# A graph attention layer: the loading queue asks for the first slab of weights when the second left half tile of x has landed instead of the first

## The chip, the cores and the metric

The kernel runs on one core of a Trainium2 chip. The metric is the device time in microseconds (us) of the whole kernel, as the median of several runs. One more run was recorded by the hardware profiler; its rows are used below.

## What is computed

x has 384 rows (nodes) of 1024 features. The reference, cut to what matters:

```python
h = jnp.maximum(_layernorm(x, axis=-1), 0.0)
q, k, v = h @ wq.T + bq, h @ wk.T + bk, h @ wv.T + bv
q2, k2, v2 = q @ wiq.T + biq, k @ wik.T + bik, v @ wiv.T + biv    # 16 heads of 64
mask = full((N, N), -inf).at[src, dst].set(softplus(edge_type_weights)[edge_type - 1])
scores = einsum('hnd,hmd->hnm', q2, k2) / 8 + mask                # diagonal always set
out = einsum('hnm,hmd->hnd', softmax(scores), v2)                 # 6528 edges
return x + out @ wo.T + bo
```

All in float32. The kernel gets the precision by splitting every operand into a rounded part ("hi") and a remainder ("lo") and doing three products, hi by hi, lo by hi and hi by lo, for each one.

## The kernel before

**Tiles and slabs.** x is three tiles of 128 rows (t = 0, 1, 2), each fetched in two half tiles of 512 columns, 256 KB each: left halves by the queue of SyncE (line 289), right halves by the queue of ScalarE (line 470). Each has its own semaphore, `x_in[t][0]` for the left and `x_in[t][1]` for the right. The seven weight matrices are 56 slabs of 128x1024 floats, 512 KB each, that go through three landing buffers (`raw`). A slab is used in order: slab 0 makes the first product tile, slab 1 the second, and so on. Each slab is first split: ScalarE writes the hi part (line 456), then VectorE (line 712) or GpSimd (line 374) writes the lo part. Slab 0 is split in halves: ScalarE makes hi of the left half (line 467), VectorE hi of the right half (line 695), GpSimd both lo parts (line 384).

**The loading queue.** SyncE does nothing but wait for semaphores and issue transfers, in program order. After the three left half tiles of x its loop over the slabs (lines 297 to 336) issues slab 0, slab 1, then five small tables (edge weights, biases, two row tables of the edges, column tables of the edges), slab 2, and two 576 KB fills of the table in memory into which the mask is scattered. From slab 3 on, the issue of a slab waits until the slab three places before it has been split (line 300). The first slab has a wait of its own (line 304): SyncE issues nothing more until a half tile of x has landed.

**The head of the kernel.** VectorE takes the statistics of each half tile (line 679) and joins those of a tile (lines 683 and 685). GpSimd turns the variance into a scale (line 367). VectorE makes the shift of tile t from it (line 626); that instruction is placed behind the statistics of the left half of tile t + 1. ScalarE normalises tiles 0 and 1 with one instruction each (line 476). Tile 2 is finished by VectorE and ScalarE in parts (lines 689, 693 and 482). TensorE turns the tiles (line 894), ScalarE and VectorE split the turned h into `a_hi` and `a_lo` (lines 486 and 725), and the first product tile (lines 922 to 929) begins. Before that TensorE does matmuls on constants to fill its time (line 890). ScalarE's order in the head is: tile 0, tile 1, hi of the left half of slab 0, tile 2, the turned h, with the hi part of slab 1 behind the fifth piece of h, and then slab 2.

**After the head.** TensorE goes through 8 product tiles for v, 8 slabs for v2, 16 tiles for q and k, 16 for q2 and k2 between the heads of the attention, and the output product. Product tile 3, for example, needs the lo part of slab 3 and the evacuated result of tile 1 (the waits in `tile`, lines 859 to 863). Beside this VectorE works out which edge wins for each cell, GpSimd scatters 51 columns of edge values and 3 of the diagonal in two chains (lines 396 and 403), and the finished mask (line 720) is first used with the first scores (line 769).

Of the kernel before, what the change touches and what calls it, by code (L numbers as in the profile page):

```python
# [66 lines left out]
def tiles_of(group):  # L67
    return range(group * EG, min((group + 1) * EG, ET))


def gat_kernel(nc, slabs, x, edge_cols, edge_rows, edge_weights, biases, bo, out):
    with ExitStack() as ctx:
# [3 lines left out]
        def sem(name):  # L76
            return ctx.enter_context(nc.semaphore(name))
# [71 lines left out]
        def key_copy(pos):  # L149

            first, n = [(work2, 0), (work2, 4), (work2, 8), (work, 0), (work, 4), (work, 8), (prob, 19), (prob, 23),
                        (prob, 3), (prob, 7), (prob, 11), (prob, 15), (prob, 0)][pos], len(tiles_of(UNIT_ORDER[pos])) * P
            flat = prob[:, :, :, :].rearrange("p a t n -> p (a t n)") if first[0] is prob else first[0]
            return flat[:, first[1] * P:first[1] * P + n]

        def cell_rows(c):

            return cells[c][0:N * N, :].rearrange("(t p n) a -> p t (n a)", p=P, n=N)
# [18 lines left out]
        x_in = [[sem(f"x_in{t}_{b}") for b in range(2)] for t in range(NT)]  # L177
# [83 lines left out]
        def wait_lo(eng, s):  # L261

            eng.wait_ge(slab_lo_dve if lo_by_vector(s) else slab_lo, lo_count(s))
# [22 lines left out]
        @block.sync  # L286
        def _(sp_eng):
            for t in range(NT):
                sp_eng.dma_start(x_sb[:, t, 0:HALF], x[t * P:(t + 1) * P, 0:HALF]).then_inc(x_in[t][0], 16)  # L289
            def load_keys(pos):  # L290

                unit = UNIT_ORDER[pos]
                part = key_rows[0:1, unit * EG * P:(unit * EG + len(tiles_of(unit))) * P]
                sp_eng.dma_start(key_copy(pos), part.to_broadcast([P, len(tiles_of(unit)) * P])).then_inc(
                    keys_in[pos], 16)

            for s in range(SLABS):
                if s >= RAW:

                    wait_lo(sp_eng, s - RAW)  # L300
                    if s == RAW:
                        sp_eng.wait_ge(half_lo, 1)
                if s == 0:
                    sp_eng.wait_ge(x_in[0][0], 16)
                sp_eng.dma_start(raw[:, s % RAW, :], slabs[s]).then_inc(slab_in[s % RAW], 16)
                if s == 1:
                    sp_eng.dma_start(ew[:], edge_weights.rearrange("(a n) -> a n", a=1).to_broadcast([P, 4])).then_inc(
                        ew_in, 16)
                    sp_eng.dma_start(bias[:], biases).then_inc(small_in, 16)
                    for i in range(2):  # L310
                        sp_eng.dma_start(rows_i[:, i, :], edge_rows[i * DST_ROW:i * DST_ROW + ET, :]).then_inc(rows_in, 16)
                    sp_eng.dma_start(cols_i[:], edge_cols).then_inc(edges_in, 16)
                if s == 2:
                    for c in range(2):
                        sp_eng.wait_ge(fill_ok, c + 1)
                        sp_eng.dma_start(cell_rows(c), prob[:, c]).then_inc(filled, 16)
                if s == 4:
                    sp_eng.wait_ge(key_row_ok, 1)
                    sp_eng.dma_start(key_rows[0, :].rearrange("(t e) -> t e", e=P), key_row[:]).then_inc(keys_out, 16)
                if 6 <= s < 4 + GROUPS:  # L320
                    if s == 6:
                        sp_eng.wait_ge(keys_out, 16)
                    elif s == 10:
                        sp_eng.wait_ge(filled, 32)
                    if s < 8:
                        load_keys(2 * (s - 6))
                        load_keys(2 * (s - 6) + 1)
                    else:
                        load_keys(s - 4)
                if s == Q0 + 2:  # L330

                    sp_eng.wait_ge(h_turned, KT)
                    sp_eng.wait_ge(later_ok, 3 * EG)
                    for t in range(NT):
                        sp_eng.dma_start(y[:, t, :], x[t * P:(t + 1) * P, :]).then_inc(y_in, 16)
                    sp_eng.dma_start(bo_sb, bo.rearrange("(a n) -> a n", a=1).to_broadcast([P, F])).then_inc(y_in, 16)
            for i, (_, n, cols_out, _) in enumerate(out_pieces):
                sp_eng.wait_ge(out_ok, i + 1)
                sp_eng.dma_start(out[n * P:(n + 1) * P, cols_out], y[:, n, cols_out]).then_inc(stored, 16)
            sp_eng.wait_ge(stored, 16 * len(out_pieces))  # L340
# [110 lines left out]
        def _(act):  # L451
# [6 lines left out]
            def tile_hi_part(t):  # L458
                hi, _, b, psum = tile_place(t)
                act.wait_ge(slab_used, slab_of(t) + 1)  # L460
                nc.scalar.activation(hi, psum[:, 0:N], ACT.Identity, bias=bias[:, b:b + 1]).then_inc(tile_hi, 1)  # L461
# [137 lines left out]
        def _(dve):  # L599
# [241 lines left out]
            for i, (_, n, cols_out, psum) in enumerate(out_pieces):  # L841
                dve.wait_ge(out_done, i + 1)
                nc.vector.tensor_tensor(y[:, n, cols_out], psum, y[:, n, cols_out], ALU.add).then_inc(out_ok, 1)
# [283 lines left out]
```

## Time and profile before

| | |
|---|---|
| median of 3 runs | 295.54 us (295.51 to 296.37) |
| the profiled execution | 295.47 us |
| its span in the trace | 293.7 us |
| TensorE busy (matmul) | 287.4 us, 98% of the span |
| TensorE's share of the chain that ended last | 95% |
| transfers' share of that chain | 2% |
| VectorE, ScalarE, GpSimd busy | 60%, 52%, 51% |
| moved by the DMA engines | 40.84 MB, 139 GB/s on the mean |
| one slab, from issue to landing | 3.4 us (median of 56) |

The span is the stretch in which the engines' instructions lie; the profiled execution's own time is 1.8 us longer. "Busy" is the time in which at least one instruction of the engine was running. The chain that ended last is followed back from the last instruction, each time to what released it, so an engine's share of it says how much of the time it decided. TensorE's granted clock was at full speed, 2.4 GHz, in the whole stretch up to the last few us.

### The profile page before, as it was taken

The page shows a single profiled execution, that of the slowest core. Times are in us where ns is not written, and L with a number is a line of the kernel's source. Part 1 is how long each engine was busy: PE and PEld are TensorE (multiplying, and loading weights), DVE is VectorE, ACT ScalarE, POOL GpSimd, SP SyncE. Part 2 cuts the span into 40 slices and gives each one's busy share as a digit, 9 for nine tenths or more (in the row PEclk, how much of TensorE's full clock was granted, in tenths as well). Part 3 has the DMA queues.
Part 4 walks back from the last instruction along what each step waited for, and adds up shares of the span by engine and source line. Part 5 has one row for each costly group of instructions (what it writes and reads, how often), then busy time and mean ns, then how long its engine had stood idle before and what let it go on. Part 6 is the DMA issues. An engine that isn't in the chain of part 4 may idle for free.

```text
span 293.7 us, 4994 instructions
## 1 busy us (share of the span) xinstructions
PE 287.4 (98%) x1813; PEld 266.4 (91%) x1813; DVE 176.7 (60%) x475; ACT 153.5 (52%) x288; POOL 150.7 (51%) x153
## 2 busy tenths in 40 slices
PE   6899999999999999999999999999999999999996
PEld 3699998888899999999999999999999997888885
DVE  4999778786544534454467766665747475835241
ACT  2876443152523443244324685969687879874100
POOL 6552455543464455545300797758393939874000
PEclk9999999999999999999999999999999999999999
DMA  7978955749733443334654043140403132400032
GB/s 257 332 230 264 315 191 180 232 153 301 270 105 117 139 143 136 91 134 145 182 193 145 0 141 106 46 144 0 145 10 136 41 106 71 144 1 2 0 143 71
DMA packets 15818, 40.84 MB, mean 139 GB/s; under 512 B 3481, under 2 KB 4914, under 8 KB 15794
## 3 DMA queue, kind: packets, MB, share of 16 engines
q1 hardware_dynamic: 13346, 38.53, 39.2%
q0 software_dynamic: 2016, 1.21, 1.8%
q10 hardware_dynamic: 432, 0.79, 0.7%
q8 instruction: 14, 0.23, 0.3%
q14 instruction: 10, 0.08, 0.1%
HBM read 37.71 MB, written 2.81 MB: 138 GB/s over the span
## 4 chain that ended last, share of the span: by engine, by line
PE 95%; DMA 2%; ACT 1%; DVE 0%; SPq 0%; issue 0%
PE banks L849 27%; PE banks L850 26%; PE banks L851 26%; PE banks L966 5%; PE banks L1009 3%; PE banks L1010 3%; PE banks L981 3%; DMA x_sb<-in_x 2%; PE banks L994 1%; PE banks L894 1%; PE banks L922 1%; PE banks L929 0%; PE banks L923 0%; ACT x_sb L476 0%; SPq L289 0%; DVE stats L679 0%
## 5 line engine op out<-in xcount | busy, mean ns | idle before, releaser
L403 POOL DMA_INDIRECT cells<-value,cell x51 | 54.8, 1074 | 59.2 <-DMA cells<-value,cell 45.9
L456 ACT ACTIVATE w_hi<-raw 128x1024 fp32r<-128x1024 f32 x51 | 53.8, 1055 | 17.5 <-PE banks L851 17.3
L849 PE MATMUL banks<-a_hi,w_hi 128*128 128x384 f32 x184 | 61.5, 334 | 0.0
L850 PE MATMUL banks<-a_hi,w_lo 128*128 128x384 f32 x184 | 61.5, 334 | 0.0
L851 PE MATMUL banks<-a_lo,w_hi 128*128 128x384 f32 x184 | 61.5, 334 | 0.0
L712 DVE TENSOR_TENSOR w_lo<-raw,w_hi 128x1024 fp32r<-128x1024 f32 x36 | 44.0, 1223 | 12.6 <-ACT w_hi L456 12.5
L429 POOL TENSOR_SCALAR prob<-prob,row_inv 128x384 f32<-128x384 f32 x36 | 22.5, 640 | 43.6 <-DVE row_inv L779 43.6
L374 POOL TENSOR_TENSOR w_lo<-raw,w_hi 128x1024 fp32r<-128x1024 f32 x15 | 36.0, 2404 | 0.9 <-ACT w_hi L456 0.9
L849 PEld LDWEIGHTS banks<-a_hi,w_hi 128*128 128x128 f32 x184 | 34.5, 188 | 0.1
L850 PEld LDWEIGHTS banks<-a_hi,w_lo 128*128 128x128 f32 x184 | 34.5, 188 | 0.0
L851 PEld LDWEIGHTS banks<-a_lo,w_hi 128*128 128x128 f32 x184 | 34.5, 188 | 0.0
L783 DVE TENSOR_TENSOR pt_lo<-banks,pt_hi 128x384 fp32r<-128x384 f32 x48 | 23.8, 551 | 13.3 <-ACT pt_hi L548 13.1
L461 ACT ACTIVATE b_hi<-banks,bias 128x384 fp32r<-128x384 f32 x16 | 9.3, 581 | 35.0 <-PE banks L851 35.0
L534 ACT ACTIVATE prob<-prob,neg_max 128x384 f32<-128x384 f32 x36 | 21.8, 606 | 9.2 <-DVE neg_max L769 9.2
L548 ACT ACTIVATE pt_hi<-banks 128x384 fp32r<-128x384 f32 x48 | 20.1, 491 | 5.6 <-PE banks L1010 4.5
L849 PE MATMUL banks<-c_hi,w_hi 128*128 128x384 f32 x64 | 22.2, 346 | 0.0
L700 DVE SCALAR_TENSOR_TENSOR b_lo<-banks,bias,b_hi 128x384 fp32r<-128x384 f32 x16 | 9.9, 617 | 20.1 <-ACT b_hi L461 20.1
L849 PE MATMUL banks<-b_hi,w_hi 128*128 128x384 f32 x64 | 21.9, 343 | 0.0
L851 PE MATMUL banks<-b_lo,w_hi 128*128 128x384 f32 x64 | 21.4, 335 | 0.0
L851 PE MATMUL banks<-c_lo,w_hi 128*128 128x384 f32 x64 | 21.4, 334 | 0.0
L850 PE MATMUL banks<-c_hi,w_lo 128*128 128x384 f32 x64 | 21.4, 334 | 0.0
L850 PE MATMUL banks<-b_hi,w_lo 128*128 128x384 f32 x64 | 21.4, 334 | 0.0
(146 smaller groups left out, 610.1 us busy)
## 6 DMA issues: line engine op xcount, KB each, us to landing
raw<-in_slabs SPq DMA_DIRECT2D x56, 512.0 KB, 3.4
work<-key_rows SPq DMA_DIRECT2D x6, 256.0 KB, 5.3
prob<-key_rows SPq DMA_DIRECT2D x6, 256.0 KB, 3.8
x_sb<-in_x SPq DMA_DIRECT2D x3, 512.0 KB, 6.0
out_y<-x_sb SPq DMA_DIRECT2D x5, 256.0 KB, 2.1
cells<-prob SPq DMA_DIRECT2D x2, 576.0 KB, 7.9
cells<-value,cell POOLq DMA_INDIRECT x51, 2.6
x_sb<-in_x ACTq DMA_DIRECT2D x3, 256.0 KB, 4.3
```

The lines of the kernel that those rows point to most:

```text
L374: nc.gpsimd.tensor_tensor(lo, raw[:, s % RAW, :], hi.bitcast(F32), ALU.subtract).then_inc(slab_lo, 1)
L403: nc.gpsimd.indirect_dma_start(out=cells[c][:, :], out_offset=bass.IndirectOffsetOnAxis(ap=cell[:, t:t + 1], axis=0), in_=value[:, t:t + 1 ...
L429: nc.gpsimd.tensor_scalar(probs[j % 2][x][:, n, :], probs[j % 2][x][:, n, :], row_inv[:, j % 2, c:c + 1], 1.0, ALU.mult, ALU.mult).then_in ...
L456: nc.scalar.activation(split_place(s)[0], raw[:, s % RAW, :], ACT.Copy).then_inc(slab_hi, 1)
L534: nc.scalar.activation(probs[j % 2][x][:, n, :], probs[j % 2][x][:, n, :], ACT.Exp, scale=-1.0, bias=neg_max[:, j % 2, c:c + 1], accum_out ...
L548: nc.scalar.activation(pt_as_placed(pt_hi, h, m), pt_place(h, m), ACT.Copy).then_inc(pt_hi_ok, 1)
L712: nc.vector.tensor_tensor(lo, raw[:, s % RAW, :], hi.bitcast(F32), ALU.subtract).then_inc(slab_lo_dve, 1)
L783: nc.vector.tensor_tensor(pt_as_placed(pt_lo, h, m), pt_place(h, m), pt_as_placed(pt_hi, h, m).bitcast(F32), ALU.subtract).then_inc(pt_lo_ ...
L849: nc.tensor.matmul(psum, w[0], a[0], start=first, stop=False)
L850: nc.tensor.matmul(psum, w[1], a[0], start=False, stop=False)
L851: return nc.tensor.matmul(psum, w[0], a[1], start=False, stop=last)
L966: mm = nc.tensor.matmul(score_bank(2 * n + x)[:, 0:N], q[own, turn, m], k[own, turn, :], start=(p == 0), stop=(p == 2))
```

## The change

In its loop over the slabs SyncE waits ahead of slab 0 on another semaphore: on that of the left half of tile 1 instead of the left half of tile 0. Nothing else changes: the same transfers are issued by the same queues in the same order.

```diff
                 if s == 0:
-                    sp_eng.wait_ge(x_in[0][0], 16)
+                    sp_eng.wait_ge(x_in[1][0], 16)
                 sp_eng.dma_start(raw[:, s % RAW, :], slabs[s]).then_inc(slab_in[s % RAW], 16)
```

## Rows read from the trace of the kernel before

**Rows 1.** Waits of TensorE in the whole span: total us, times, longest.
```profile
PE banks L894 <- ACT x_sb L476: 0.9, 2, 0.6
PE banks L922 <- ACT a_hi L486: 0.2, 1, 0.2
```

**Rows 2.** Chain that ended last, its head: start us, us, what.
```profile
1.70 6.04 DMA x_sb<-in_x
12.10 0.41 PE banks L922
```

**Rows 3.** Timeline of SyncE's queue, the head: start us, us, instruction.
```profile
3.97 0.80 SPq L305 DMA_DIRECT2D raw<-in_slabs  x2
...
7.27 0.43 SPq L305 DMA_DIRECT2D raw<-in_slabs  x1
7.75 0.96 SPq L316 DMA_DIRECT2D cells<-prob  x2
13.68 3.60 SPq L305 DMA_DIRECT2D raw<-in_slabs  x2
```

**Rows 4.** DMA issues: x left of tile 1 (1.2 us), of tile 2 (1.7 us); last, us to landing.
```profile
x_sb<-in_x SPq DMA_DIRECT2D x1, 256.0 KB, 4.2
...
x_sb<-in_x SPq DMA_DIRECT2D x1, 256.0 KB, 6.0
```

**Rows 5.** DMA issues: slabs 0, 2, 3, 4 (issued at 4.0, 7.3, 13.7, 17.0 us); second fill.
```profile
raw<-in_slabs SPq DMA_DIRECT2D x1, 512.0 KB, 5.1
...
raw<-in_slabs SPq DMA_DIRECT2D x1, 512.0 KB, 6.6
...
raw<-in_slabs SPq DMA_DIRECT2D x1, 512.0 KB, 4.2
...
raw<-in_slabs SPq DMA_DIRECT2D x1, 512.0 KB, 3.3
...
cells<-prob SPq DMA_DIRECT2D x1, 576.0 KB, 8.5
```

**Rows 6.** Busy time by stretch; last three columns: granted clock, DMA share, GB/s moved.
```profile
1.00:7.00 6.00, 4.55 (x18) 2.24 (x18) 2.86 (x7) 1.70 (x2) 4.13 (x13) 1.00 0.83 288
7.00:7.74 0.74, 0.32 (x2) 0.00 (x0) 0.52 (x3) 0.74 (x1) 0.07 (x1) 1.00 1.06 418
```

**Rows 7.** Timeline of VectorE, the head and first use of the mask.
```profile
7.76 0.69 DVE L679 BATCH_NORM_STATS2 stats<-x_sb 128x6 f32<-128x512 f32 x1 [0.18 <-DMA x_sb<-in_x]
8.37 0.14 DVE L626 SCALAR_TENSOR_TENSOR shift<-mean_var,rstd 128x1 f32<-128x1 f32 x1
...
16.24 0.69 DVE L618 TENSOR_SCALAR sp<-ew 128x4 f32<-128x4 f32 x1
...
23.34 0.62 DVE L700 SCALAR_TENSOR_TENSOR b_lo<-banks,bias,b_hi 128x384 fp32r<-128x384 f32 x1
...
152.75 1.36 DVE L720 SCALAR_TENSOR_TENSOR work<-prob 128x1152 f32<-128x1152 f32 x1
...
159.33 0.55 DVE L769 CUSTOM_DVE_ANT_0 prob<-banks,work 128x384 f32<-128x384 f32 x1
```

**Rows 8.** Timeline of GpSimd, second tile's scale and first scatter.
```profile
7.67 0.55 POOL L367 TENSOR_TENSOR rstd<-var_eps,minus_half 128x1 f32<-128x1 f32 x1 [1.31 <-DVE var_eps L685]
...
22.30 1.26 POOL L396 DMA_INDIRECT cells<-sp,self_cell  x1 [3.20 <-issue]
```

**Rows 9.** Timeline of ScalarE, the instructions that read slabs 0 to 3.
```profile
9.70 0.62 ACT L467 ACTIVATE w_hi<-raw 128x512 fp32r<-128x512 f32 x1
...
13.33 1.10 ACT L456 ACTIVATE w_hi<-raw 128x1024 fp32r<-128x1024 f32 x1
...
15.39 1.13 ACT L456 ACTIVATE w_hi<-raw 128x1024 fp32r<-128x1024 f32 x1
...
17.93 1.06 ACT L456 ACTIVATE w_hi<-raw 128x1024 fp32r<-128x1024 f32 x1
```

**Rows 10.** Timeline of TensorE, the first matmul of product tile 3.
```profile
25.43 0.33 PE L849 MATMUL banks<-a_hi,w_hi 128*128 128x384 f32 x1
```

## Prediction

> **What bounds the kernel now.** I read the page first (TensorE busy 98% of the span, 95% of the chain that ended last), then the waits of TensorE, the head of the chain in order of time, the timelines of the five engines in the first 30 us, the DMA issues one by one, and the transfer rate by stretch. TensorE's waits say where the time can still be moved. In the whole span TensorE waits for another engine's data only in the head: twice for the normalised tiles, 0.9 us together, and once, 0.2 us, for the turned h [rows 1]. The first real product starts at 12.10 us [rows 2], and no row of a wait starts behind it. So the kernel is a head of 12.1 us and then a body in which TensorE never stops. A change to the loading order counts only if it moves the 12.10, or if it makes a slab, a table or the mask so late that TensorE gets a wait that it has not now.
>
> The head's chain begins with the left half of tile 2 of x: its transfer is the chain's longest piece, from 1.70 to 7.74 us [rows 2]. But VectorE had only been free for 0.18 us when it landed [rows 7]: the chain names this transfer, and just behind it stands VectorE's own work.
>
> **The moved wait.** SyncE issues slab 0 at 3.97 us, when the left half of tile 0 has landed [rows 3]. The left half of tile 1 was issued at 1.2 us and took 4.2 us [rows 4], so it landed at 5.4. The whole queue behind the wait moves by 5.4 - 3.97 = 1.4 us: slabs 0 and 1, five transfers of small tables, slab 2 and two fills, ten issues in all, the last of which now ends at 7.75 + 0.96 = 8.7 us [rows 3] and then at 10.1. Slab 3 is issued at 13.68, released by the split of slab 0, so SyncE itself has caught up by then and its issue does not move. One wait replaces another, so no instruction is added.
>
> **What it can gain.** Up to 7.00 us the DMA engines moved 6.00 x 288 = 1.73 MB and to 7.74 another 0.31 MB [rows 6], 2.04 MB together. x is 6 x 0.262 = 1.57 MB. So at least 0.47 MB of slabs had moved before the last left half tile of x had landed. If all of that were in the way, x would land 0.47 MB / 418 GB/s = 1.1 us sooner, at 6.6. VectorE can use 0.18 us of it. Then the shift of tile 1, which releases ScalarE's tile 1, needs the scale of GpSimd, ready at 7.67 + 0.55 = 8.22 [rows 8]; it runs at 8.37 now [rows 7] and could at 8.26, with the 0.04 us that a hand-over takes. So the head gains 0.11 us at the most. That it gains nothing is the other end, and nothing here makes the last left half later. The order of landing favours this end: the slabs' bytes stand behind x's in the same queue. Slab 0 landed at 3.97 + 5.1 = 9.1 [rows 5], 1.4 us after the last left half tile, and 512 KB at the 418 GB/s of this stretch are 1.25 us. The slab thus went behind x's last piece, not beside it; early bytes of slabs passed on DMA engines that were done with their share of x, and those had nothing else to do. I take 0, with 0.11 as the bound.
>
> The Trainium skill has this as a rule: DMA: Bandwidth & Descriptors, "Queues, rings and completion order", says that each DMA engine takes one queue's descriptors in ring order and takes turns between queues. By that rule a slab on SyncE's queue can hold up only the right half tiles on ScalarE's queue, not the left half that the chain names, so the sum would be 0; by the plain count of bytes it would be 0.11. The landing 1.4 us apart agrees with the rule; no row of before shows one DMA engine's turns by themselves.
>
> **What it can cost: slab 0.** Its first reader on ScalarE starts at 9.70 us, straight behind tile 1 and without a wait [rows 9]. The margin now is 0.6 us. With the request at 5.4, a slab with nothing before it takes 3.3 us (slab 4) [rows 5] and lands at 8.7. With the 5.1 us of slab 0 itself it lands at 10.5, and with the 6.6 us of slab 2 [rows 5], which stood behind seven other transfers, at 12.0. I go by what it stands behind: before, its 5.1 us held the 3.8 us until x's last left half landed (7.74 - 3.97), and then its own 1.4. That end of x does not move, so slab 0 lands at about 9.1 again, in the middle of 8.7 and 9.7. No cost. Without this cover each us behind 9.70 goes one to one into ScalarE's order, hence into the turned tile 2, the first half of the weights' lo part and the 12.10: 10.5 would cost 0.8 us.
>
> **Slabs 1 and 2 and the tables.** Slab 1 was issued some 0.4 us behind slab 0; with even the 6.6 us of slab 2 and 1.4 us of shift it is there at 4.4 + 6.6 + 1.4 = 12.4, and ScalarE reads it at 13.33 [rows 9]. Slab 2 landed at 7.27 + 6.6 = 13.9 and is read at 15.39 [rows 9]; shifted in full it lands at 15.3, just in time. The small tables stand ahead of slab 2 in the queue, so they are there by 15.3 too, before VectorE's 16.24 [rows 7], the first reader among them. All cost 0; cover left for slab 2 is 0.1 us, but TensorE needs its product only at the end of tile 1, some 4 us further.
>
> **Fills, slab 3 and the mask.** The second fill landed at 8.2 + 8.5 = 16.7 [rows 5] and lands at 18.1 at the latest, against the first scatter at 22.30 [rows 8]. Slab 3 took 4.2 us behind the fills [rows 5], landed at 17.9, and ScalarE's 17.93 [rows 9] reads it at once: here is no cover, and ScalarE may be held for 1.4 us. What stands behind it is a table load, the logarithm, the split of slab 3's lo part and, on VectorE, the edge values and the evacuation of tile 1 at 23.34 + 0.62 = 23.96 [rows 7]. TensorE wants that evacuation at 25.43, with product tile 3 [rows 10]. So 1.5 us of cover stands against 1.4 us: cost 0, or 0.1 at the worst. The edge work goes to the mask, finished at 152.75 + 1.36 = 154.1 and first used at 159.33 [rows 7]: 5.2 us of cover for the same 1.4.
>
> **The sum.** The profiled execution took 295.47 us (span 293.7 and 1.8 around it). 295.47 - 0 + 0 = 295.47; the median of the runs is 295.54, 0.07 above. I say 295.5.
>
> **The rivals.** (a) The left half of tile 2 really shares its way with the slabs and comes earlier: the head is 0.11 us shorter, 295.4. For it speaks that 0.47 MB of slabs moved before x was in; against it, the landing of slab 0 behind x. (b) Slower: slab 0 misses ScalarE's 9.70. Its place is line 467 in ScalarE's order, its price is the landing less 9.70, and it decides from 9.70 on; it is a slowdown that can be told only when slab 0 lands behind 10.6. With 5.1 us from request to landing the time is 295.54 + 0.8 = 296.3, with 6.6 us (12.0) it is 297.8. For it speaks that a request costs a fixed time that the queue now no longer hides; against it, that slab 4's 3.3 us end at 8.7. (c) The late queue reaches TensorE in the body: slab 2's 0.1 us and slab 3's missing cover add up on ScalarE and VectorE, and product tile 3 waits for the evacuation of tile 1. With 1.4 us of shift this is 0.1 us, 295.6; only a shift of 2.4 us would make it 1.0 us, and nothing lengthens it to that. (d) Faster by more than 0.11 us would need a wait of TensorE other than those 1.1 us in the head, and there is none.
>
> **How the numbers follow.** Forecast, with nothing moved by more than 0.05 us: 0.50. (a) 0.23. (b) 0.15, of which 0.07 below 296.4 and 0.08 above. (c) 0.07. (d) or something that I don't see on the faster side: 0.05. A difference of 0.3%, 0.9 us, is about what a measurement of this kernel can tell from no change. The forecast, (a), (c) and the near part of (b) lie within it: 0.50 + 0.23 + 0.07 + 0.07 = 0.87; faster 0.05, slower 0.08. The range goes from 295.0, for (a) and the 0.3 us by which medians of short series part, to 296.4, which holds (b) at 5.1 us and the highest of the three runs, 296.37.
>
> **What would show it.** In the profile after, SyncE issues slab 0 at 5.4. Right: the left half of tile 2 lands at 7.7 and VectorE still waits for it 0.1 to 0.2 us; slab 0 lands at about 9.1; ScalarE's line 467 starts at 9.7 with no idle time; the first product starts at 12.1; slab 3's hi part starts 0 to 1.4 us behind 17.93, and TensorE has no wait behind the head. (a) is shown by a VectorE without that wait and a first product at 12.0. (b) is shown by ScalarE idle ahead of line 467 for a transfer. (c) is shown by a wait of line 849 at about 25.4. The forecast is wrong if the first product starts more than 0.9 us from 12.1, or if TensorE gets a wait in the body.

## The result and the profile after

The changed kernel took 296.50 us in the median of 22 runs (295.37 to 302.12), the kernel before 295.48 us in the median of 22 (295.31 to 296.37). The ratio is 1.0027, with a 95% interval of 1.0019 to 1.0035: slower by 0.8 us, just inside what I had called no change, but clearly not zero, and the median lies 0.1 us above the range. Executions that were 1.5% or more above the fastest of their kernel, as the 302.12 was, are in the medians but neither in the ratios nor in the counts of the table below. The profiled execution took 296.48 us (span 294.8), against 295.47 us before: 1.0 us more.

The medians hide one thing. The runs of before lie within 0.3 us of each other but for one; those of the changed kernel, without the 302.12, lie anywhere between 295.4 and 297.8, 12 of 21 above 296. The change made a margin so thin that chance decides from run to run.

What decided the profiled run stands in the chain that ended last, its head (start us, us, what), where before one transfer of x stood [rows 2]:

```profile
1.24 4.20 DMA x_sb<-in_x
...
5.45 5.58 DMA raw<-in_slabs
...
11.06 0.64 ACT w_hi L467
...
11.77 1.28 POOL w_lo L384
...
13.14 0.41 PE banks L922
```

The chain now goes from the left half of tile 1 over SyncE's request to slab 0, and from it through the split of slab 0's left half. The first product starts at 13.14 us instead of 12.10 [rows 2]: the 1.0 us of the profiled execution is all there. SyncE's queue in the profile after, to be read against [rows 3]:

```profile
5.45 0.80 SPq L305 DMA_DIRECT2D raw<-in_slabs  x2
...
9.57 0.43 SPq L305 DMA_DIRECT2D raw<-in_slabs  x1
10.05 0.96 SPq L316 DMA_DIRECT2D cells<-prob  x2
14.32 4.00 SPq L305 DMA_DIRECT2D raw<-in_slabs  x2
```

Slab 0 is asked for at 5.45, as worked out; slab 2 is 2.3 us later than before, not 1.5, since the issues of the tables took longer. The DMA issues after (last figure: us from issue to landing), the last left half tile of x and slab 0, against [rows 4] and [rows 5]:

```profile
x_sb<-in_x SPq DMA_DIRECT2D x1, 256.0 KB, 5.5
...
raw<-in_slabs SPq DMA_DIRECT2D x1, 512.0 KB, 5.6
```

x came 0.5 us sooner (5.5 instead of 6.0 us), and slab 0 landed at 5.45 + 5.6 = 11.0 us. The busy time by stretch after (last columns: granted clock, DMA share, GB/s), against [rows 6]:

```profile
1.00:7.00 6.00, 4.55 (x15) 2.21 (x16) 2.79 (x7) 1.63 (x2) 4.13 (x13) 1.00 0.85 277
7.00:7.74 0.74, 0.74 (x5) 0.27 (x3) 0.67 (x4) 0.74 (x1) 0.01 (x1) 1.00 0.57 205
```

In the second stretch the DMA engines moved 205 GB/s where they had moved 418 [rows 6]: x was nearly through, and the slab was not yet coming. VectorE, ScalarE and TensorE after, against [rows 7] and [rows 9]:

```profile
7.57 0.68 DVE L679 BATCH_NORM_STATS2 stats<-x_sb 128x6 f32<-128x512 f32 x1
```
```profile
8.51 1.24 ACT L476 ACTIVATE x_sb<-x_sb,shift,rstd 128x1024 f32<-128x1024 f32 x1 [0.62 <-DVE shift L626]
11.06 0.63 ACT L467 ACTIVATE w_hi<-raw 128x512 fp32r<-128x512 f32 x1 [1.30 <-DMA raw<-in_slabs]
```
```profile
12.14 0.84 PE L894 MATMUL banks<-ident,x_sb 128*128 128x128 f32 x4 [0.86 <-ACT x_sb L482]
13.14 0.41 PE L922 MATMUL banks<-a_hi,w_hi 128*128 128x384 f32 x1 [0.16 <-POOL w_lo L384]
```

VectorE's wait for the last left half is gone, and ScalarE's tile 1 comes a little sooner. Then ScalarE stands idle 1.30 us for slab 0, in front of tile 2 of x, whose scale GpSimd had ready at 10.35 us.

### The profile page after: what moved, and what is told of

Same layout as the page of the kernel before. It is cut to its first block, busy times and chain, and to the rows that moved or that the text cites. A ratio compares the mean times of both kernels' runs of the same rounds, so it can differ in the third digit from the quotient of the medians.

```text
span 294.8 us, 4994 instructions
## 1 busy us (share of the span) xinstructions
PE 288.2 (98%) x1813; PEld 266.5 (90%) x1813; DVE 175.7 (60%) x475; ACT 153.7 (52%) x288; POOL 150.2 (51%) x153
## 4 chain that ended last, share of the span: by engine, by line
PE 95%; DMA 3%; POOL 0%; ACT 0%; DVE 0%; SPq 0%; issue 0%
PE banks L849 27%; PE banks L850 26%; PE banks L851 26%; PE banks L966 5%; PE banks L1009 3%; PE banks L1010 3%; PE banks L981 3%; DMA raw<-in_slabs 2%; DMA x_sb<-in_x 1%; PE banks L994 1%; PE banks L922 1%; PE banks L929 0%; PE banks L923 0%; POOL w_lo L384 0%; PE banks L894 0%; ACT w_hi L467 0%
```

## The experiments

Each kernel was timed in five rounds beside the kernel before on the same chip; its runs are compared with those of before in the same series (medians 295.46 us in the first, 295.46 in the second, 295.41 in the third). The shape of the runs says more here than the median, so the table has it too. "Scatter short" means that the last 4 scatters of each of the two chains are left out (8 of 54 columns), so the mask is ready long before its use.

| kernel | slab 0 asked for behind | the rest of the queue behind | scatter | median us | above 296 / above 297.5 / runs counted |
|---|---|---|---|---|---|
| the change, first | left half of tile 1 | slab 0 | whole | 296.50 | 12 / 1 / 21 |
| again, series 1 | tile 1 | slab 0 | whole | 296.64 | 6 / 1 / 8 |
| again, series 3 | tile 1 | slab 0 | whole | 295.78 | 4 / 0 / 11 |
| rest late | tile 0 | tile 1 | whole | 295.35 | 0 / 0 / 11 |
| wait tile 2 | tile 2 | slab 0 | whole | 296.56 | 8 / 1 / 8 |
| no wait | nothing | slab 0 | whole | 295.87 | 2 / 1 / 11 |
| short, series 2 | tile 1 | slab 0 | short | 295.51 | 3 / 0 / 12 |
| short, series 3 | tile 1 | slab 0 | short | 296.39 | 5 / 2 / 9 |
| tile 2, short | tile 2 | slab 0 | short | 296.61 | 5 / 0 / 5 |
| rest later | tile 0 | tile 2 | whole | 295.65 | 3 / 3 / 12 |
| rest later, short | tile 0 | tile 2 | short | 295.58 | 0 / 0 / 11 |
| halves | tile 1, in two halves | slab 0 | whole | 295.86 | 5 / 2 / 11 |
| scatter delay | tile 0 | slab 0 | whole, held up | 295.52 | 3 / 2 / 12 |

The counts fall into two bands. Between 296 and 297.5 us lie 20 of 40 runs of the change and 6 of 21 of the change with the scatter short, but none of the 34 of the three kernels that ask for slab 0 as before and hold the rest back. So this band goes with slab 0's request. The runs above 297.5 also occur with slab 0 early.

Line numbers in rows are those of each kernel, up to six higher or two lower than before behind an edit. Theory A: slab 0 lands too late for ScalarE's line 467, and this is the loss. Theory B, and in a sharper form theory M: the rest of the queue is late, and the loss is in the body.

**The change once more.** No edit.

> The changed kernel once more, for the spread of slab 0's landing. Theory A (slab 0's landing sets the loss, line 467 of ScalarE waits for it): the time is 296.0 to 297.0, and in the profile the first product (line 922) starts at slab 0's landing plus 2.1 us where that landing is behind 9.6 us, at 12.0 where it is not. Rival B (the late tables, fills and slab 3 make the loss in the body): the first product starts at 12.0 to 12.1 in some profile and the time is 1 us above before all the same.

The profiled run took 295.84 us, and in it slab 0 was in time:

```profile
9.84 0.62 ACT L467 ACTIVATE w_hi<-raw 128x512 fp32r<-128x512 f32 x1
```
```profile
12.24 0.41 PE L922 MATMUL banks<-a_hi,w_hi 128*128 128x384 f32 x1 [0.22 <-ACT a_hi L486]
```

The first product is at 12.24. ScalarE's instruction was not held, though the landing records put slab 0 at 9.68 us, behind the 9.6 from which A had let it cost.

This and the first profile are one kernel with two landings, and the difference in time follows the landing, as A says. But 3 of all 10 runs lie above 297.5, more than slab 0 explained in any profile so far. The ratio is 1.0043 (1.0023 to 1.0063). The third series ran the same kernel again on another chip: 295.78 us, where I had expected 296.2 to 296.7 for both theories together, and a ratio of 1.001 (0.998 to 1.004), so that series alone does not tell the change from before. In its profile slab 0 landed at 9.96 us and the first product started at 12.20.

**Only what follows slab 0 is late.**

```diff
-                if s == 0:
-                    sp_eng.wait_ge(x_in[1][0], 16)
+                if s < 2:
+                    sp_eng.wait_ge(x_in[s][0], 16)
```

> Slab 0 is asked for as before (left half of tile 0 landed), and slab 1 with everything behind it as in the change (left half of tile 1 landed). Theory A: slab 0 lands at 9.1 or sooner, line 467 does not wait, and the time is that of before, 295.4 to 295.6 (ratio 1.000). Rival B: the 1.4 us by which tables, fills, slab 1 and slab 2 are late are kept, so the loss stays, 296.3 or more. If taking slab 1 out of the way of x also helps x: the last left half lands 0.2 to 0.5 us sooner and the head is 0.1 us shorter.

Measured: 295.35 us, ratio 0.9992 (0.998 to 1.0004), all 11 runs between 295.20 and 295.72. The loss is gone with the early request of slab 0 alone, while slab 1 and the rest still wait for tile 1. A holds, and B does not at this lateness; the tables go out at 5.76 us here and at 6.30 in the change, so the rest is some 0.5 us less late. VectorE's wait for x is gone here too:

```profile
7.64 0.68 DVE L679 BATCH_NORM_STATS2 stats<-x_sb 128x6 f32<-128x512 f32 x1
```

That would be the 0.1 us of my rival (a), too small to be told from nothing in the times. Whether the later requests bring it, this profile does not show: the last experiment has the loading queue of before, and VectorE has no wait for x there either.

**Slab 0 asked for behind tile 2.**

```diff
-                    sp_eng.wait_ge(x_in[1][0], 16)
+                    sp_eng.wait_ge(x_in[2][0], 16)
```

> SyncE asks for slab 0 only when the left half of tile 2 has landed (about 7.2 us). Rival C (slab 0 took 5.6 us in the changed kernel because the last half tiles of x were in front of it): the request is answered in 3.3 us, slab 0 lands at 10.5, the loss is about 0.9 us, no more than in the change. Rival D (a first request behind x takes 5 to 5.6 us wherever it stands): it lands at 12.3 to 12.8 and the loss is 2.7 to 3.2 us, 298.2 to 298.7. Theory A expects first product = landing + 2.1 in both.

Measured: 296.56 us, ratio 1.0031 (1.002 to 1.0041), no run below 296.0. In the profile SyncE asks at 6.81 and slab 0 is read 3.2 us later, so rival C is right and D wrong: with x through, a slab takes 3.2 us. Most of that is not data, which is 1.3 us at 400 GB/s; right behind the request the DMA engines move nothing (last columns: granted clock, DMA share, GB/s):

```profile
7.00:7.74 0.74, 0.28 (x2) 0.00 (x0) 0.67 (x4) 0.74 (x1) 0.00 (x0) 1.00 0.00 0
```

ScalarE and TensorE in this run:

```profile
10.04 0.63 ACT L467 ACTIVATE w_hi<-raw 128x512 fp32r<-128x512 f32 x1 [0.26 <-DMA raw<-in_slabs]
```
```profile
12.12 0.43 PE L922 MATMUL banks<-a_hi,w_hi 128*128 128x384 f32 x1 [0.16 <-POOL w_lo L384]
```

The head of this run lost nothing, and yet it took 298.76 us. Here are TensorE's waits in it (total us, times, longest), and VectorE's for the mask:

```profile
PE banks L966 <- DVE k_lo L700: 2.3, 1, 2.3
...
PE banks L849 <- DVE b_lo L700: 0.6, 1, 0.6
```
```profile
156.92 1.36 DVE L717 SCALAR_TENSOR_TENSOR prob<-prob,work 128x1152 f32<-128x1152 f32 x1 [4.91 <-DMA prob<-cells]
```

TensorE has 2.9 us of waits in the body, at two places. The first scores wait 2.3 us for a k2 tile whose evacuation stands in VectorE's order behind the mask, and VectorE waited 4.91 us for the mask. The other 0.6 us have nothing to do with the mask. They are my rival (c), product tile 3 waiting for the evacuation of tile 1, which ended at 26.13 us (25.51 + 0.62) and not at 23.96 [rows 7]:

```profile
26.27 0.41 PE L849 MATMUL banks<-a_hi,w_hi 128*128 128x384 f32 x1 [0.64 <-DVE b_lo L700]
```

VectorE's wait for the mask was there already in the profile before, though short:

```profile
151.35 1.36 DVE L717 SCALAR_TENSOR_TENSOR prob<-prob,work 128x1152 f32<-128x1152 f32 x1 [0.27 <-DMA prob<-cells]
```

So the mask is another place for a loss, and theory M was made from it.

**No wait at all.** The line is taken out.

> No wait ahead of slab 0: it and all behind it are issued from 2.1 us on, straight behind x. If slabs hold up x: the last left half of x lands behind the 7.7 us of before, and each us of it goes into the head, up to 1 us (296.5). If the slabs only fill what x leaves (my forecast's reading, by which nothing of x changed): it lands at 7.7, slab 0 at about 9, and the time is 295.5.

Measured: 295.87 us, ratio 1.0015 (1.0001 to 1.0029). With slabs issued from 2.1 us on, it is the right half of tile 2, on ScalarE's queue, that suffers. The DMA issues of tile 2's halves, left then right, and VectorE's statistics of the right half:

```profile
x_sb<-in_x SPq DMA_DIRECT2D x1, 256.0 KB, 5.9
x_sb<-in_x ACTq DMA_DIRECT2D x1, 256.0 KB, 7.4
```
```profile
9.12 0.69 DVE L677 BATCH_NORM_STATS2 stats<-x_sb 128x6 f32<-128x512 f32 x1 [0.69 <-DMA x_sb<-in_x]
```

So slabs do hold up x, but on the other queue; the left half ahead of them in their own queue came as before (5.9 us for 6.0). The first product is at 12.73. The wait that the change moved has two sides: without it x is late, with more of it slab 0 is.

**The change with the scatter short**, in two series.

```diff
-            while done < 2 * CHAIN:
+            while done < 2 * (CHAIN - 4):
...
+            pool.wait_ge(cell_ok, GROUPS)
             for c in range(2):
-                pool.wait_ge(scattered[c], 16 * CHAIN)
+                pool.wait_ge(scattered[c], 16 * (CHAIN - 4))
```

The added wait holds GpSimd until VectorE has made the cells of the last group, for which the scatters left out waited before.

> The changed kernel with the last 4 scatters of each of the two chains left out (8 of the 54 columns of edge and diagonal values, so the mask lacks them); the mask is ready some 16 us sooner and cannot be late. Theory A (slab 0's landing, through ScalarE's line 467, makes the loss in the head): nothing changes, 296.2 to 296.8, ratio 1.002 to 1.005, with the same spread of runs from 295.4 to 297. Theory M (the mask comes late, VectorE waits for it and TensorE for VectorE, as in one profile of the request behind tile 2): the loss goes away, 295.4 to 295.6 in nearly all runs.

> The changed kernel with the last 4 scatters of each chain left out (8 of 54 columns), on the same chip. Theory A+M: only the head's part is left; runs between 295.4 and 297.2, none above 297.5, more of them below 295.8 than in the changed kernel. Theory A alone: the same distribution as the changed kernel.

Measured: 295.51 us (3 of 12 above 296) and 296.39 us (5 of 9 above 296, and two at 298.6 and 298.8). The first looks like M, the second like A, and the last two runs break what I had expected of both together, no run above 297.5. A kernel whose mask cannot be late still has runs 3.4 us above before, though one of the 32 runs of before on that chip, at 299.69, lies as high. Both runs have a mean granted clock of TensorE of 0.994, and so has the 299.69 of before; in every run below 298.5 us of which the clock is on record it is 0.998 or more. The missing 0.6% of a span of 295 us is 1.8 us, an estimate of what the lower clock took, and it would put the two runs near 297. Of the 13 runs of the change and the experiments above 298.5 us ten have 0.994 or less, so the highest times are not to be read as waits alone. The profiled run, at 295.45, shows a ScalarE that waits 0.31 us for slab 0 with next to no loss. What held up the runs above it, or lowered their clock, no profile shows.

**Tile 2 with the scatter short.**

> Slab 0 asked for behind the left half of tile 2, and the last 4 scatters of each chain left out as above. The profile with the whole mask had 0.3 us of loss in the head (slab 0 landed at 10.0) and 2.9 us behind, where TensorE waited for VectorE and VectorE 4.9 us for the mask. Theory M: without the mask's lateness only the head's part is left, 295.6 to 296.1, and the runs above 298 are gone. Theory A: the median stays at 296.5, since slab 0 lands 1 us late in most runs.

Measured: 296.61 us, five runs between 296.17 and 296.76. The runs near 299 and 301 of the whole mask are gone, but with five runs here that says little. The 1.1 us in the median are not gone. The profile shows 0.8 of them in the head and 0.3 at the place of rival (c):

```profile
10.83 0.63 ACT L468 ACTIVATE w_hi<-raw 128x512 fp32r<-128x512 f32 x1 [0.98 <-DMA raw<-in_slabs]
```
```profile
12.91 0.41 PE L923 MATMUL banks<-a_hi,w_hi 128*128 128x384 f32 x1 [0.16 <-POOL w_lo L384]
```
```profile
PE banks L850 <- DVE b_lo L701: 0.3, 1, 0.3
```

From line 467's start to the first product it is 13.14 - 11.06 = 2.08 us in the change, 12.12 - 10.04 = 2.08 with the request behind tile 2, and 12.91 - 10.83 = 2.08 here. In these three profiles, in which slab 0 decides, the first product is 2.1 us behind its landing.

**Slab 0 early, the rest behind tile 2**, with the scatter whole and short.

```diff
-                if s == 0:
-                    sp_eng.wait_ge(x_in[1][0], 16)
+                if s < 2:
+                    sp_eng.wait_ge(x_in[2 * s][0], 16)
```

> Slab 0 asked for as before, all that follows it (slabs 1 and 2, tables, fills) only when the left half of tile 2 has landed, later than in the changed kernel. Theory A: the head is untouched, ScalarE's line 467 does not wait, 295.4 to 295.6. Theory M: tables and fills are up to 2.5 us late, the edge keys and the first scatter with them, the mask is late, and the loss is as large as in the change or larger, 296.5 or more.

> Slab 0 asked for as before, all behind it when the left half of tile 2 has landed, and the last 4 scatters of each chain left out (8 of 54 columns). With the whole mask 9 of 12 runs were at 295.4 to 295.7 and 3 at 297.8 to 299.1. Theory A+M: both causes are gone, so all runs lie at 295.2 to 295.8. Theory A with something else late in the body (slab 3, tables): the runs at 298 remain.

Measured: with the whole scatter 9 of 12 runs at 295.37 to 295.73 and three at 297.80, 298.06 and 299.06; with the short one all 11 runs between 295.32 and 295.84. With slab 0 early and the mask safe no high run is left, although slabs 1 and 2, tables and fills are all later than in the change. The three high runs, 2.3 to 3.6 us above before, stand against none of 11 once the mask is safe, on two chips. That points to the mask and does not show it: none of the three was profiled, and in the profiled run VectorE waits only 0.19 us for the mask.

**Slab 0 in two halves.**

```diff
                     sp_eng.wait_ge(x_in[1][0], 16)
+                    sp_eng.dma_start(raw[:, 0, 0:HALF], slabs[0][:, 0:HALF]).then_inc(left_in, 16)
+                    sp_eng.dma_start(raw[:, 0, HALF:F], slabs[0][:, HALF:F]).then_inc(slab_in[0], 16)
+                    continue
...
-                act.wait_ge(slab_in[0], 16)
+                act.wait_ge(left_in, 16)
```

> The changed kernel with slab 0 fetched as two halves of 256 KB, the left one first and with a semaphore of its own, on which line 467 waits. Theory A: the left half lands some 0.7 us before the whole slab did, the first product starts up to that much sooner, and the time is 0.3 to 0.7 us below the change (295.8 to 296.2). Theory M: no difference from the change, or a little more from one more issue, 296.5.

Measured: 295.86 us, six runs at 295.31 to 295.48 and six from 296.24 to 299.88. The half of the runs without a loss fits A. Of the head there is one profile, and it is mended there: the left half landed at 9.10 us, and ScalarE read it at 9.63 without a wait. The profiled one, 297.46 us, is the second mechanism by itself. Its head, its wait of TensorE, its last scatter and VectorE at the mask:

```profile
12.03 0.41 PE L926 MATMUL banks<-a_hi,w_hi 128*128 128x384 f32 x1 [0.22 <-ACT a_hi L490]
```
```profile
PE banks L970 <- DVE k_lo L704: 1.5, 1, 1.5
```
```profile
144.07 1.20 POOL L407 DMA_INDIRECT cells<-value,cell  x1 [1.69 <-DMA cells<-value,cell]
...
155.33 1.36 DVE L721 SCALAR_TENSOR_TENSOR prob<-prob,work 128x1152 f32<-128x1152 f32 x1 [4.13 <-DMA prob<-cells]
```

The first product is 0.07 us ahead of before. The first scatter started at 23.67 us, 1.4 behind the 22.30 of before [rows 8]. The last one started at 144.07, and 139.88 before:

```profile
139.88 1.12 POOL L403 DMA_INDIRECT cells<-value,cell  x1 [1.78 <-DMA cells<-value,cell]
```

A slip of 1.4 us at the start has become 4.2 at the end. It need not: with slab 0 early and the rest behind tile 2 the first scatter started at 23.71 us, as late as here, the last one at 141.47, and VectorE waited 0.19 us for the mask. So a late start is not the whole cause; something along the chain added 2.8 us here, and no run shows what.

**The kernel before, with the scatter chains held up** and the loading queue untouched.

```diff
+                if done == 1:
+                    pool.wait_ge(cell_ok, 1)
+                    for i in range(4):
+                        nc.gpsimd.memset(iota[:], 0.0).then_inc(idle_ok, 1)
+                        pool.wait_ge(idle_ok, i + 1)
                 scatter(done // 2, done % 2)
```

> The kernel before, with four small memsets (on a tile that is no longer used) on GpSimd between the first and second scatter, which hold the two scatter chains up by some 1.7 us; the loading queue is untouched. Theory M with a delay handed on one to one: the mask comes 1.7 us later, VectorE waits 2 us and TensorE, which has about 2 us in hand there, not at all or a few tenths: 295.4 to 295.8. Theory M with a delay that can grow in the chain (in one profile a start 1.4 us late made an end 4.2 us late): some runs at 297 to 299 beside others at 295.5. Theory A alone: 295.5 in all runs.

Measured: 295.52 us; nine of 12 runs at 295.36 to 295.57, and 296.69, 298.05 and 299.36. The second scatter started at 30.88, 1.7 us behind the 29.16 of before, as meant:

```profile
28.53 1.85 POOL L422 MEMSET iota<- 128x384 f16 x4 [4.89 <-DVE cell L656]
30.88 0.99 POOL L404 DMA_INDIRECT cells<-value,cell  x1 [0.50 <-POOL iota L422]
...
141.43 0.96 POOL L404 DMA_INDIRECT cells<-value,cell  x1 [0.30 <-issue]
```

This gives the same picture as the late rest of the queue: mostly nothing, in a quarter of the runs 1 to 4 us (the 299.36 with a granted clock of 0.993). But the ratio of 1.0024 has an interval of 0.9999 to 1.0048, one of the 32 runs of before on this chip is as high, and in the profiled run the mask is not late. VectorE takes it up without a wait:

```profile
151.13 1.35 DVE L723 SCALAR_TENSOR_TENSOR prob<-prob,work 128x1152 f32<-128x1152 f32 x1
```

So a late start of the chains may be enough for the high runs, and that is not shown.

This run has a second use, since its loading queue is that of before. The left half of tile 2 of x, and VectorE's statistics of it:

```profile
x_sb<-in_x SPq DMA_DIRECT2D x1, 256.0 KB, 5.5
```
```profile
7.73 0.69 DVE L685 BATCH_NORM_STATS2 stats<-x_sb 128x6 f32<-128x512 f32 x1
```

It took 5.5 us, as in the change, and VectorE did not wait for it.

## Why the prediction was wrong

- **The frame was right.** TensorE is the bound from the first product on, and only a later first product or a new wait in the body could cost. The first happened in the profiled run of the change, the second in three profiles of experiments. (Of TensorE's waits I had left out 2.5 us at line 890 for a constant from GpSimd; they lie ahead of the matmuls that only fill time.)
- **The moved wait** was at 5.45, as worked out. The issue of slab 3, which I had fixed at 13.68, came at 14.32, since the split of slab 0 that releases it was late.
- **The gain** can't be told. I took 0 for the last left half tile, with 0.11 us as the bound. In the profile after it came 0.5 us sooner, VectorE's wait went away, and tile 1 on ScalarE started 4.47 us behind VectorE's first instruction (8.51 and 4.04), not 4.57 (8.55 and 3.98). That looks like rival (a), with a gain of 0.1 us that is lost again before it reaches TensorE. But the kernel with the scatter chains held up, whose loading queue is that of before, has 5.5 us, no wait and 4.47 us too (8.68 and 4.21). Over the profiles the left half took 5.3 to 5.6 us with slab 0's request as in the change (six), 5.5, 5.6, 6.0, 6.0 and 6.1 us with it as before (five), and 5.1 and 5.8 us with it behind tile 2: a tendency towards (a), and no more. The Trainium skill (DMA: Bandwidth & Descriptors, "Queues, rings and completion order") says that each DMA engine takes a queue's descriptors in ring order and takes turns between the queues, and I had read from it that the slab cannot hold up the left half in its own queue. The run with no wait agrees with it (left half 5.9 us, right half on the other queue 7.4, for 6.0 and 6.2 before); the tendency speaks against it.
- **The step that failed** is in "What it can cost: slab 0": "That end of x does not move, so slab 0 lands at about 9.1 again". It landed at 11.0. I had split the 5.1 us of before into 3.8 behind x and 1.4 of its own, and kept the landing fixed to the end of x. But a request has a time of its own before its first byte: behind tile 2, asked for at 6.81, nothing moved from 7.00 to 7.74. Before, this time ran while x was still coming. In the change the DMA engines were half empty at 7.0 to 7.7 us, 205 GB/s for 418. With the request where the change has it, slab 0 landed at 9.4, 9.7, 10.0, 10.1 and 11.0 us in the five profiles that there are of it (landing records of the traces), never at the 8.7 of the lower bound. So (b), which had 0.15, had the mechanism. The profiled 11.0 lies between its 10.5 and 12.0, and the other four lie between my 9.1 and its 10.5. In the profiled run twelve of the 16 parts of slab 0 were there at 9.6, which would have cost nothing; four late parts made the 11.0, and I had no term for them. The pass to TensorE I had priced at one to one from 9.70; it is one to one from about 10.0 (12.12 - 2.08), since GpSimd, which makes the lo part behind line 467, has tile 2's scale in hand until 10.38 (9.63 + 0.75 before). So 11.06 costs 1.04 us.
- **The fills, slab 3 and the mask** failed as well, in a way that the median hides. I took the mask's deadline to be its first use at 159.33 us [rows 7] and gave it 5.2 us of cover. Its deadline is VectorE's own place for it. VectorE waited for it already before, and all of VectorE's order stands behind it. Waits of 4.91 and 4.13 us there cost TensorE 2.3 and 1.5 us, so the cover is 2.6 us and not 5.2. And I let a slip pass one to one along 54 scatters, where 1.4 us became 4.2 in one profile and 1.6 in another. Rival (c) was right about its place: with the request behind tile 2, 2.8 us later than before, product tile 3 waited 0.6 us for the evacuation of tile 1. In the change's own profiles it did not.
- **The range** ended at 296.4 because the late landings of slab 0, 10.5 and 12.0, had too little weight, and because I took the spread of the changed kernel's runs to be that of before. This kernel lost its margin and gained spread.

What stays open: how much of the 0.8 us belongs to each cause. The profiled run has all of its loss in the head. But 22 of 40 counted runs of the change lie above 296, and 8 of 21 with the scatter short, which is not enough to tell them apart, and chips differ. Open too is why slab 0 takes 3.9 us from its request in one execution and 5.6 in another, what lets the scatter chains slip, and what lowers the granted clock in the highest runs.

## What to carry to other kernels

A request has an answer time, and part of it hides behind the transfers that are still running when it is made. When you move the request, charge the whole answer time from the new request, and do not tie the landing to the end of the transfer in front. To take the place of a wait, ask which of the requests behind it has the least margin and leave that one alone: holding the rest of the queue back behind tile 1, and not slab 0, cost nothing in 11 runs here, while holding it back behind tile 2 left three of 12 runs high. The gain that the change was made for, 0.1 us, can't be measured in the times. The deadline of a result is the place of its consumer in the consuming engine's order, not its first use on the bounding engine, and the delay of a long chain of dependent transfers need not stay what it was at the start. A median hides such things; the shape of the runs showed them.

## What the runs showed of the hardware

A 512 KB slab asked for when x was all but through landed 3.2 and 3.3 us later (two profiles of the request behind tile 2). Asked for behind tile 1, at 5.3 to 5.6 us, it took 3.9 to 4.8 us in four profiles and 5.6 in one: there the earlier request had the later landing, 11.0 for 10.0 us. By the landing records of that trace, one for each of the 16 parts of a transfer, 11 of the 16 parts of slab 0 were there between 8.4 and 9.0 us, one at 9.6, and the last four between 10.9 and 11.04. A transfer is as late as its latest parts, and four of 16 decided 1.0 us of the kernel.

The chain of scatters has no one pace. Where the whole chain ran, the last scatter started at 139.8 to 140.5 us in five profiles (before among them), and in the other five at 141.4, 141.5, 142.3, 144.1 and 144.7, from first starts that lay within 2.2 us of each other (22.3 to 24.5). From nearly the same first start, 23.67 and 23.71, the last one came at 144.1 and at 141.5.
